# State-space block of a decoder: products and scans over both channel halves at once, and the output rows broadcast by DMA

## The reference, cut to what matters

```
xz = layernorm(x) @ W_in;  x_in, z = split(xz)            # 256 channels each
xc = silu(causal_conv4(x_in) + conv_b)
dt_r, Bm, Cm = split(xc @ W_xproj)                        # 8, 16 and 16 columns
dt = softplus(dt_r @ W_dt + b_dt);  A = -exp(A_log)       # A is [256, 16]
h[t,d,n] = h[t-1,d,n]*exp(dt[t,d]*A[d,n]) + dt[t,d]*Bm[t,n]*xc[t,d]
y[t,d] = sum_n h[t,d,n]*Cm[t,n] + xc[t,d]*D[d]
out = x + (y*silu(z)) @ W_out
```

## Time and profile before

| what | us |
|---|---|
| median of 3 runs | 1950.89 |
| span of the profiled execution | 1948.6 |
| state-space block, first product to last gate | 707.74 to 1287.98 |
| VectorE busy in 780 to 852 | 67.89 of 72 |
| TensorE, GpSimd, ScalarE busy there | 58.90, 52.10, 48.40 |

### The profile page before, as it was taken

How to read it: one execution, slowest core, us unless ns; L and a number is a source line. 1 busy time by engine, 2 the same in 40 slices (tenths; PEclk the granted TensorE clock), 3 DMA queues, 4 the chain that set the end, 5 groups by cost and what they waited for, 6 DMA issues and landing times. The chain is left out here.

```text
span 1948.6 us, 31799 instructions
## 1 busy us (share of the span) xinstructions
PE 1562.9 (80%) x10219; PEld 1017.4 (52%) x10219; DVE 1491.3 (77%) x2947; ACT 953.5 (49%) x1491; POOL 920.7 (47%) x938
## 2 busy tenths in 40 slices
PE   8889888989699978977878878769998811699991
PEld 4545547988476632322333333236776611588891
DVE  6899986887488779999989999967777678533335
ACT  3545543575544567657656666436566410011114
POOL 4455442444200147677676677654344100366653
PEclk8999998999899989999988999979999855799996
DMA  4000000000000000000000000020000040466654
GB/s 144 2 0 0 0 1 27 2 2 1 12 1 0 1 1 1 1 1 0 0 1 0 0 0 1 1 78 11 5 9 5 3 145 0 159 209 206 212 171 135
DMA packets 49075, 75.34 MB, mean 39 GB/s; under 512 B 8861, under 2 KB 34821, under 8 KB 48437
## 3 DMA queue, kind: packets, MB, share of 16 engines
q1 hardware_dynamic: 43541, 64.12, 10.5%
q0 software_dynamic: 4544, 9.32, 1.6%
q10 hardware_dynamic: 864, 0.33, 0.1%
HBM read 62.26 MB, written 11.48 MB: 38 GB/s over the span
## 5 line engine op out<-in xcount | busy, mean ns | idle before, releaser
L1506 POOL TENSOR_TENSOR m_hC<-m_h,m_Cs 128x512 f32<-128x512 f32 x256 | 328.2, 1287 | 169.2 <-DVE m_h L1680 122.6
L1788 PE MATMUL PS<-m_hC,identf 128*128 128x512 f32 x512 | 296.5, 662 | 100.9 <-POOL m_hC L1506 99.9
L1680 DVE TENSOR_TENSOR_SCAN m_h<-m_dA,PS 128x512 f32<-128x512 f32 x256 | 312.4, 1220 | 11.2
L1788 PEld LDWEIGHTS PS<-m_hC,identf 128*128 128x128 f32 x512 | 93.0, 203 | 236.4 <-POOL m_hC L1506 208.9
L1675 DVE TENSOR_TENSOR PS<-PS,m_DU 128x512 f32<-128x512 f32 x256 | 178.4, 697 | 19.9 <-issue 3.8
L1616 ACT ACTIVATE m_dA<-m_DT,m_A 128x508 f32<-128x508 f32 x256 | 174.3, 714 | 31.3 <-DVE m_DT L1664 31.1
L1996 ACT ACTIVATE e_Sg<-PS 128x512 f32<-128x512 f32 x71 | 42.4, 597 | 223.0 <-PE PS L2238 178.8
L2238 PE MATMUL PS<-e_xT,e_WT 128*128 128x128 f32 x1136 | 143.8, 281 | 4.9 <-DVE e_xT L2146 3.4
L1608 ACT COPY m_Cs<-PS 128x512 f32<-128x512 f32 x128 | 73.7, 576 | 143.7 <-PE PS L1766 143.5
L2238 PEld LDWEIGHTS PS<-e_xT,e_WT 128*128 128x128 f32 x1136 | 135.4, 195 | 9.3 <-DVE e_xT L2146 7.1
L1935 POOL DMA_INDIRECT e_XG<-token_rows,e_ids x71 | 68.8, 969 | 138.9 <-DVE e_ids L2140 117.6
(11 more groups left out here) (411 smaller groups left out, 3801.6 us busy)
## 6 DMA issues: line engine op xcount, KB each, us to landing
e_WT<-in_w_wgu SPq DMA_DIRECT2D x71, 512.0 KB
token_rows<-X SPq DMA_DIRECT2D x2, 2048.0 KB
e_Y<-expert_rows SPq DMA_DIRECT2D x16, 256.0 KB, 4.0
k_BD<-in_w_bcr SPq DMA_DIRECT2D x1, 2464.0 KB, 9.5
e_w_wd<-in_w_wd SPq DMA_DIRECT2D x1, 2048.0 KB, 7.9
out_dram<-X SPq DMA_DIRECT2D x8, 256.0 KB, 2.4
X<-in_x SPq DMA_DIRECT2D x1, 1792.0 KB, 8.7
x_Cs<-in_ctx SPq DMA_DIRECT2D x8, 154.0 KB
```

The lines of the kernel that those rows point to most:

```text
L1506: nc.gpsimd.tensor_tensor(hC[:, i % ND, :], hst[:, i % ND, :], Cs[:, n % ND, :], ALU.mult).then_inc(s["hC"], 1)
L1680: nc.vector.tensor_tensor_scan(hst[:, i % ND, :], dA[:, i % NA].rearrange("p b l -> p (b l)"), bank(4), 0.0, ALU.mult, ALU.add).then_inc(s ...
L1788: nc.tensor.matmul(bank(5 + ch), c.identf[:, :], hC[:, i % ND, :], start=False, stop=(n == NS - 1)).then_inc(s["yacc"], 1)
```

## The change

The step loops keep their 32 step numbers, but one instruction serves both channel halves:

- VectorE: at ch 0 one product of 2 x 512 columns (B's row broadcast over the halves) into banks 3 and 4; at ch 1 one scan of 1024 columns. The first product of a group waits for both halves of DU. The two gates become one of 1024 columns.
- GpSimd: nothing at ch 0; at ch 1 one product of 1024 columns. `hC` has 2 buffers of 1024 columns (`NY`), `h` has 4 of 1024 (`ND`).
- TensorE: C's spreads are gone; B's spread for n + 2 is issued at ch 0. The identity matmuls remain, two per n, and both wait for the product of both halves.
- ScalarE: the copies of C are gone; `parts` copies 104 rows instead of 8.
- SyncE: stores C's 16 rows of each group to DRAM and, for each n, loads row n back into all 128 partitions (256 KB written to SBUF), 4 buffers (`NC`).
- Slots: gate 1 to 2, output0 1 to 4, output1 3 to 5, stats and rstd 6 to 7, silu_z (last group only) 3 to 1, last_c gone. The others keep theirs.

```diff
-    ND, NA = 4, 8
+    ND, NA, NC, NY = 4, 8, 4, 2
-    SLOT = {"last_c": 0, "gate": 1, "output0": 1, "silu_z": 3, "output1": 3, "rstd": 6, "stats": 6, ...
+    SLOT = {"gate": 2, "output0": 4, "silu_z": 1, "output1": 5, "rstd": 7, "stats": 7, ...
@@ SyncE
+            def store_c(g):
+                sp.wait_ge(s["dtr"], g + 1)
+                sp.dma_start(c.CD[g, :, :], rows[NS:2 * NS, :]).then_inc(s["cd"], 16)
+                sp.wait_ge(s["cd"], 16 * (g + 1))
+            store_c(0)
+            for g in range(NG):
+                for n in range(NS):
+                    if g > 0 or n >= NC:
+                        sp.wait_ge(s["hC"], g * NS + n - NC + 1)
+                    sp.dma_start(Cs[:, n % NC, :], c.CD[g, n:n + 1, :].to_broadcast([P, T])).then_inc(landed[n % NC], 16)
+                if g + 1 < NG:
+                    store_c(g + 1)
@@ GpSimd
-                nc.gpsimd.tensor_tensor(hC[:, i % ND, :], hst[:, i % ND, :], Cs[:, n % ND, :], ALU.mult)
+                if ch == 0:
+                    return
+                pool.wait_ge(s["h"], g * NS + n + 1)
+                pool.wait_ge(landed[n % NC], g * (16 * NS // NC) + 16 * (n // NC + 1))
+                nc.gpsimd.tensor_tensor(hC[:, n % NY], hst[:, n % ND], Cs[:, n % NC, :]...to_broadcast([P, CH, T]), ALU.mult)
@@ VectorE
+                if ch == 0:
+                    if n == 0:
+                        dve.wait_ge(s["du"], g * CH + CH)
+                    nc.vector.tensor_tensor(PS[:, 3:5, :], bank(1 + n % 2)...to_broadcast([P, CH, T]), DU[:, par], ALU.mult)
+                else:
+                    nc.vector.tensor_tensor_scan(hst[:, n % ND]..., dA[:, at:at + CH]..., PS[:, 3:5, :]..., 0.0, ALU.mult, ALU.add)
@@ TensorE
                 if ch == 0:
-                    if n + 1 < NS:
-                        spread_c(g, par, n + 1)
+                    if n + 2 < NS:
+                        spread_b(g, par, n + 2)
-                pe.wait_ge(s["hC"], g * NI + i + 1)
+                pe.wait_ge(s["hC"], g * NS + n + 1)
```

More of the change, by code:

```diff
@@ L1420, in state_space @@
     YG = sb("YG", [P, CH, T])
-    dtr = sb("dtr", [104, T])
+    rows = sb("rows", [104, T])
     R = sb("R", [96, T])
@@ L1432, in state_space @@
     bl = lambda ap: ap.rearrange("p (b l) -> p b l", b=GB)
-    SLOT = {"last_c": 0, "gate": 1, "output0": 1, "silu_z": 3, "output1": 3, "rstd": 6, "stats": 6, "norm": 11, "x0": 8, "x1": 9, "x2": 11, "inner_stats": 11,
+    SLOT = {"gate": 2, "output0": 4, "silu_z": 1, "output1": 5, "rstd": 7, "stats": 7, "norm": 11, "x0": 8, "x1": 9, "x2": 11, "inner_stats": 11,
             "inner_rstd": 11, "x3": 13, "dt_b_c": 14, "dt0": 15, "inner_norm": 16, "silus": 18, "rest": 18, "dt1": 18, "parts": 19, "last": 20,
@@ L1570, in parts @@
                 act.wait_ge(s["bcp"], g + 1)
-                nc.scalar.copy(dtr[96:104, :], PS[96:104, 0, :]).then_inc(s["dtr"], 1)
+                if not isinstance(g, int) or g > 0:
+                    act.wait_ge(s["cd"], 16 * g)
+                nc.scalar.copy(rows[:, :], PS[0:104, 0, :]).then_inc(s["dtr"], 1)
                 nc.scalar.copy(hi[:, par, :], bank(0, 96)).then_inc(s["hi"], 1)
@@ L1602, in logs @@
                 nc.scalar.activation(E2[:, :, :], E2[:, :, :], ACT.Copy, bias=-1.0).then_inc(s["c1"], 1)
[L1604 to L1608, removed]
             def step(g, par, i, left):
@@ L1614, in step @@
                 if not first(g, i, NA):
-                    act.wait_ge(s["h"], g * NI + i - NA + 1)
+                    act.wait_ge(s["h"], g * NS + n - NA // CH + 1)
                 nc.scalar.activation(dA[:, i % NA, :, 1:P], bl(DT[:, par, ch, :])[:, :, 1:P], ACT.Exp, scale=A[:, ch, n:n + 1]).then_inc(s["dA"], 1)
[L1617 to L1625, removed]
             def norm(g, par):
@@ L1684, in gate @@
                 dve.wait_ge(s["sz"], g + 1)
-                for ch in range(CH):
-                    nc.vector.tensor_tensor(YG[:, ch, :], bank(5 + ch), SZ[:, par, ch, :], ALU.mult).then_inc(s["y1"], 1)
+                nc.vector.tensor_tensor(YG[:, :, :], PS[:, 5:7, :], SZ[:, par], ALU.mult).then_inc(s["y1"], 1)
             def out_stats(g, par):
@@ L1757, in spread_b @@
                 if not first(g, n, 2):
-                    pe.wait_ge(s["dBu"], g * NI + CH * (n - 1))
+                    pe.wait_ge(s["dBu"], g * NS + n - 1)
                 nc.tensor.matmul(bank(1 + n % 2), W["sel"][:, n:n + 1].to_broadcast([96, P]), hi[:, par, :], start=True, stop=True).then_inc(s["B"], 1)
[L1761 to L1766, removed]
             def step(g, par, i, left):
```

58 lines of the change are left out of this document (26 added, 32 removed).

## The result

The changed kernel takes 2008.84 us (median of 4 runs, 2007.13 to 2010.54), the kernel before 1951.93 beside it: ratio 1.0286, 95% interval 1.0269 to 1.0304. The direction was as forecast, the size was not: 1975 was said, with 1930 to 1997 as the range. The profiled span is 2005.4 us. From the first product to the last gate it now takes 634.7 us (708.80 to 1343.50) against 580.2 and against 603.5 forecast; what lies outside went from 1368.4 to 1370.7. So all of the loss but 2.3 us is in the block, and so is the miss: 31 of 34 us.

What follows compares the result with a forecast made beforehand. VectorE's pace bounds the block, hand-offs just hidden. Products and scans gain 51.5 us, but stalls of 12.2 us per group (85.4 in seven) and other waits move the last gate by +24.6: 1975 us, range 1930 to 1997.

Steps and rivals of the forecast that it cites:

- Stalls 1, 2 and 3: VectorE's waits in each group before stats (3.5 us), before rest (3.1 us) and before softplus0 (2.6 us).
- stall 4: VectorE's wait before a group's first product, for both halves of DU from GpSimd: 1.1 us per group.
- I take 1.85, since that wait is the longest: TensorE's low clock at state 4, after stall 1's idle time: 1.85 us per group, bounds 0 and 4.6.
- rival C: TensorE's clock falls in every lull: 14.9 us of stalls per group, +43.5, so 1994 us; chance 0.15.
- third stretch: VectorE's time in a group from rest to softplus0; the forecast's counts give 20.6 us.
- fourth stretch: VectorE's time in a group from softplus0 to the gate; the forecast's counts give 15.0 us.
- both fall beside 512-column stages of GpSimd, so I take 0 (bounds 0 and 15 us): Shared SBUF port: VectorE's softpluses, twice per group, lose nothing to GpSimd's longer products; taken at 0.
- gaps, as now: VectorE's gaps between product, scan and next product stay 0.03 + 0.11 us, within 3.65 us per n.
- a state takes more than 3.75 us where nothing waits: Sign that the forecast is wrong: VectorE's product-and-scan pace, put at 3.65 us, exceeds 3.75 without waits.
- A: Rival: preparing chain keeps up, stalls 4.6 us per group, 1922 us; chance 0.25 including what lies towards B.
- B: Rival: gain and stalls cancel, 9 us of stalls per group, +2, so 1953 us; chance 0.12.
- D: Rival: DMA broadcasts don't land in time and GpSimd waits, +250 us, so 2200 us; chance 0.03.

Runs made afterwards that it cites:

- e2: The changed kernel with TensorE's output0 and output1 at steps 2 and 3 instead of 4 and 5: 1966.58 us, ratio 1.0066.
- e4: The changed kernel with GpSimd's product as two of 512 columns, each signalling, TensorE's pairs each waiting for their own half: 1959.56 us, ratio 1.0028.
- after: The changed kernel itself, as profiled, against the kernel before: 2008.84 us, ratio 1.0286.
- e5: The changed kernel with each spread of B issued four times into the same bank instead of once: 2006.5 us, ratio 1.0277.
- e3: The changed kernel with GpSimd's 1024-column product as two of 512 and one signal after the second: 2004.04 us, ratio 1.025.
- e6: The kernel before with only C's rows by DMA instead of by TensorE and ScalarE: 1949.83 us, ratio 0.9977.

## Why the prediction was wrong in size

**Right.** What bounds the block (VectorE's pace, with hand-offs just hidden) and the exchange: less work, longer hand-offs. Product 1.230, scan 2.284, GpSimd's product 2.378 us, as forecast. A state where nothing waits takes 3.66 us wherever the program is written out. Stalls 1, 2 and 3 stand where they were put, released by the engines named, at means of 3.4, 2.8 and 2.9 us. The last gate's wait is 4.50 us for 4.8 forecast. e2 shows stall 1 by its going away, e4 the cause of all three, the time from scan to TensorE's pair.

**Right sum by luck.** Stalls, last gate and issue had been put at 85.4 + 4.8 + 3.8 = 94, and VectorE's waits in the block, without a scan's pauses for its product (11.2), come to 93. But that 94 held 7 x 1.1 for stall 4 and 3.8 for issue; these were 1.4 (once, in the first group) and 0.6. The gates but the last (6.7) and B (11.6) stand in their place. The second softplus is so long that DU's second half is ready when VectorE is. And what VectorE lost inside its own instructions, 23.5 us, is in no wait at all.

**The step that failed first: "I take 1.85, since that wait is the longest".** The low level was counted once per group, ahead of stall 2, and it came three times. At state 4 it cost 2.66 us over what was counted, at `dt1` up to 1.9 in six of the seven groups (1.5 on average), and at the gate it made VectorE wait 0.9 on average. This is rival C's mechanism in all three of its places, priced there at 1.85, 1.7 and 1.1. The third stretch shows the second place: 22.5 us against 20.6 forecast, and 21.0 both in after's one group without it and in e5. The fourth stretch shows the third place, by after's one group without it (16.5 us for 17.5 to 17.8) and by e3. The length of TensorE's wait alone does not tell when the level falls: 2.45 us at 1244.94 was followed by the low one, 2.53 us at 918.32 by the high one. What decides stays open here. The Trainium skill, "TensorE: Matmul & The Clock Gate" (section on the clock gate), says that the throttled state is the default; the trace agrees in so far as the low level follows stretches in which TensorE did little, three times in most groups.

Of the 5.2 us by which a group missed, the first stretch is 0.35. The second is 0.45, with 0.8 more of the clock than forecast. The third is 1.9: 1.5 by the clock, 0.4 by two matmul pairs counted too short. The fourth is 2.5: 1.6 by the port, net of stall 4, and 0.9 by the clock. All three in sum: the clock 3.2 us a group over the forecast, the port 1.6.

**The step that failed on the port: "both fall beside 512-column stages of GpSimd, so I take 0 (bounds 0 and 15 us)".** The softplus that starts at 1268.58 falls beside the 1024-column product of 1268.49. `last`, which the step did not count at all, meets one too: in the second group GpSimd's product ended at 835.92 and the `last` of 834.78 at 836.47. Softpluses and `last` together cost VectorE 16.5 + 7.0 = 23.5 us more than before, beyond even the upper bound. The bound was drawn from "1.1 us longer, twice per group"; the second softplus lost 1.9 and `last` 1.0. What `last` lost came out of the wait before softplus0. The chain of the group felt the two softpluses as 2.7 us over the forecast in the fourth stretch, less the 1.1 of stall 4: 1.6 us a group. The Trainium skill, "SBUF — State Buffer" (its part on the shared port pair), says that whichever of a VectorE instruction with two SBUF operands and a GpSimd instruction starts first holds the pair for its whole length. The ends 0.55 us after GpSimd's, e3's 0.68, and the 2.81 us on GpSimd's own side all agree. The forecast weighed the rule and set it aside, and the row that it set against it, 1.23 us at 838.98, was that very effect at 512 columns: the second softplus of the same group, at 846.0 in the kernel before, took 0.74.

**The third, without effect: "gaps, as now".** The distance from product to scan is 0.15 us longer in the loop than forecast, so "a state takes more than 3.75 us where nothing waits" came true, at 3.81. By the written-out group it does not set the group's length. What makes it depend on the order of waits, and on whether their counts are constants, stays open.

**The rivals.** A (the chain keeps up, 1922) is false: `rest` and softplus0 wait every time. So is B. D is false: GpSimd never waited for a DMA in the block, and SyncE's own waits are all for GpSimd's product. C came nearest (1994 against 2008.8), and its mechanism is the larger part of the miss. What it lacked is the port.

## What to carry to other kernels

When an instruction on the bounding engine is made twice as wide, add up what the next engines must now wait for before they may start. Here VectorE's products and scans became 41 us shorter and its waits grew from 19.5 to 104 us, and letting the consumer start on the first half (e4 against e3) made the block 46 us shorter. A stall that leaves TensorE idle (2.45, 2.98 and 4.37 us here) should be priced with the slow matmuls that may follow it on the chain, each time it occurs and not only at the longest one. And a VectorE operation that reads two SBUF tiles ended here about 0.55 us after the GpSimd instruction that it met; look for where they meet before calling the port free.

## What the hardware showed that was not expected

- Small VectorE instructions between SBUF tiles grow with the width of GpSimd's: `last`, 32 rows, from 0.68 to 1.69 us, a softplus from 0.75 to 2.65. In e3 and at 1263.27 in after, GpSimd's lost about 0.5 us in turn.
- The distance from a product's start to its scan's, with nothing else in the way, is 1.27, 1.36 or 1.42 us, by the order of the same three waits and by whether they stand in a loop.
- Raising the granted clock from 0.84 to 0.92 by extra matmuls (e5) moved the time by nothing that can be measured.
- Behind waits of TensorE of nearly the same length, 2.45 and 2.53 us, the same pair of matmuls took 1.79 us once and 1.13 once.
- Broadcasting one row of 2 KB to 128 partitions, 128 times, 256 KB each, beside everything else delayed nothing, and with it alone the kernel was 0.23% faster (e6).
